# Attention output projections with every load begun at once, and attention cores whose first loads stand ahead of the clearing

## The reference

```python
attn = jax.nn.softmax(attn.astype(jnp.float32), axis=-1).astype(q.dtype)
ctx = jnp.einsum('bhqk,bhkd->bhqd', attn, v)
ctx = ctx.transpose(0, 2, 1, 3).reshape(B, N, D)
return ctx @ Wo + bo          # layer 1: out @ w_o.T * hid ** (-0.5), no bias
```

## Time and profile before

| what | value |
|---|---|
| median of 3 runs | 3518.85 us (3512.96 to 3518.86) |
| the profiled execution | 3530.75 us, its span 3529.0 us |
| mean granted TensorE clock | 0.886 of full speed |
| busy over the span | PE 77%, DVE 71%, ACT 52%, POOL 25% |
| first attention core | 125.1 to 802.4 us |
| first output projection | 807.15 to 855.77 us |
| second attention core | 1270.7 to 1947.3 us |
| second output projection | 1951.97 to 2000.73 us |

### The profile page before, as it was taken

One profiled execution on the slowest core, in us unless ns is written; L12 is line 12 of the kernel. 1 busy time (PEld: TensorE's weight loads), 2 busy tenths in 40 slices (PEclk: granted clock), 3 DMA queues, 4 the chain that ended last, 5 costly groups with the idle time before them and its releaser, 6 DMA issues. The chain is left out here.

```text
span 3529.0 us, 43620 instructions
## 1 busy us (share of the span) xinstructions
PE 2701.9 (77%) x12690; PEld 967.9 (27%) x12690; DVE 2505.7 (71%) x2942; ACT 1823.1 (52%) x3161; POOL 882.6 (25%) x985
## 2 busy tenths in 40 slices
PE   6499999984469649999998424867777777996666
PEld 3022222221136412222222114622222232332222
DVE  4699999963236469999996271288999975446548
ACT  2188888881224128888888102355555531224233
POOL 3311111100446221111110006416777740000000
PEclk8599999996789759999999657987999998998878
DMA  4200101003522330100100312111000000001010
GB/s 120 91 24 23 28 23 28 23 15 89 90 70 67 106 117 24 28 24 24 27 23 15 102 35 74 48 51 38 6 12 12 7 0 1 0 0 59 6 42 24
DMA packets 161483, 140.96 MB, mean 40 GB/s; under 512 B 51941, under 2 KB 135781, under 8 KB 160984
## 3 DMA queue, kind: packets, MB, share of 16 engines
q1 hardware_dynamic: 142040, 98.68, 10.5%
q0 software_dynamic: 19328, 40.87, 3.8%
HBM read 73.85 MB, written 65.62 MB: 40 GB/s over the span
## 5 line engine op out<-in xcount | busy, mean ns | idle before, releaser
L640 DVE TENSOR_REDUCE a_att_mx<-a_att_s 128x2 f32<-128x1024 f32 x1024 | 1204.9, 1219 | 77.8 <-PE a_att_s L551 65.7
L625 ACT ACTIVATE a_att_pt<-a_att_st 128x512 f32<-128x512 f32 x2048 | 1064.5, 603 | 246.9 <-PE a_att_st L577 246.3
L577 PE MATMUL a_att_st<-a_att_qst,a_att_kst 50*128 50x512 bf16 x2048 | 620.7, 385 | 63.9 <-ACT a_att_pt L625 51.6
L551 PE MATMUL a_att_s<-a_att_kst,a_att_qst 50*128 50x512 bf16 x2048 | 524.8, 399 | 85.1 <-DMA a_att_kst<-a_kstk 52.2
L564 PE MATMUL a_att_av<-a_att_pt,a_att_vst 128*32 128x512 f32 x4096 | 547.2, 607 | 0.0
L577 PEld LDWEIGHTS a_att_st<-a_att_qst,a_att_kst 50*128 50x128 bf16 x2048 | 157.9, 94 | 727.1 <-ACT a_att_pt L625 668.7
L2191 POOL TENSOR_TENSOR g_xn<-m2s_hs,m2s_cb 128x1024 f32<-128x1024 f32 x128 | 300.8, 2355 | 119.0 <-DVE m2s_hs L2158 68.7
L2158 DVE TENSOR_TENSOR_SCAN m2s_hs<-m2s_da,m2s_bps 128x1024 f32<-128x1024 f32 x128 | 292.7, 2287 | 4.4
L487 POOL CAST a_att_mt_in<-a_att_nmax 128x16 bf16<-128x16 f32 x64 | 12.6, 196 | 1072.7 <-DVE a_att_nmax L648 1072.7
L2074 PE MATMUL m2s_yps<-g_xn,g_ident 128*128 128x512 f32 x512 | 242.8, 597 | 0.9
L2130 ACT COPY m2s_cb<-m2s_cps 128x1024 f32<-128x1024 f32 x128 | 129.5, 1012 | 184.1 <-POOL g_xn L2191 182.5
(11 more groups left out here) (477 smaller groups left out, 3681.5 us busy)
## 6 DMA issues: line engine op xcount, KB each, us to landing
a_att_qst<-a_qstk POOLq DMA_DIRECT2D x128, 100.0 KB, 2.5
a_att_kst<-a_kstk POOLq DMA_DIRECT2D x128, 100.0 KB, 2.6
a_qstk<-a_qkv_part SPq DMA_DIRECT2D x96, 128.0 KB, 1.9
a_kstk<-a_qkv_part SPq DMA_DIRECT2D x96, 128.0 KB, 2.0
f_xs<-f_sent SPq DMA_DIRECT2D x20, 396.0 KB, 5.8
f_sent<-f0r_zero SPq DMA_DIRECT2D x1, 5148.0 KB, 22.7
a_num<-a_att_oev SPq DMA_DIRECT2D x256, 16.0 KB
a_out_nm<-a_num SPq DMA_DIRECT2D x16, 256.0 KB, 3.4
```

Source lines behind the costliest of these rows:

```text
L551: mm = pe.matmul(s1[:, cut % 2, h, :], qst[u][64 * h:64 * h + STACK, qt * P:(qt + 1) * P], kst[u][64 * h:64 * h + STACK, kh * CH:(kh + 1) ...
L577: pe.matmul(st[:, e % 3, :], kst[u][64 * h:64 * h + STACK, kt * P:(kt + 1) * P], qst[u][64 * h:64 * h + STACK, half * CH:(half + 1) * CH], ...
L625: act.activation(pt[:, e % 16, :], st[:, e % 3, :], ACT.Exp, scale=scale).then_inc(exp_done, 1)
L640: dve.tensor_reduce(mx[:, par, 2 * cut:2 * cut + 2], s1[:, cut % 2, :, :], AX.X, ALU.max).then_inc(s1_used, 1)
```

## The change

1. Output projection. `nm` and `cx` are gone; the numerators are loaded into `g.xn` by four transfers of 1024 tokens each (512 KB), issued by ScalarE, whose stream was empty in this stage. They wait for nothing. `rb` has a buffer for every chunk, and SP issues its 8 loads one behind the other, with no wait between them, once the reciprocals are stored. The loop is written out. DVE multiplies in place in `g.xn` and does the addition of chunk c-2 behind the multiplication of chunk c; PE has 4 PSUM banks where it had 2. Each load has its own semaphore: the stage has 18 where it had 8.
2. Attention core. Two of pair 0's four stacks (head 0's) are loaded by SP, the other two and those of pairs 1 and 2 by POOL at the very start, ahead of the clearing of `vst`; the three copies of values stand behind the clearing. PE's first cut waits for SP's two on a semaphore of their own and for POOL's two on `ldq[0]`.

```diff
@@ attention_stage
+                for hp in range(3):
+                    for h in range(2):
+                        if hp > 0 or h == 1:
+                            stacks(pool, 0, hp, h, ldq[hp])
                 for u in range(4):
                     pool.memset(vst[u][:, :, :, :], 0.0).then_inc(vset, 1)
...
                 for hp in range(3):
-                    fetch(0, hp, None)
+                    values(0, hp)
...
+                stacks(sp, 0, 0, 0, ldq_first)
                 for n in range(2):
                     rows(n, n, 16 * (n // 2 + 1))
...
                     if cut == 0:
-                        pe.wait_ge(ldq[u], 64 * rounds)
+                        if isinstance(n, int) and n == 0:
+                            pe.wait_ge(ldq_first, 32)
+                        pe.wait_ge(ldq[u], 64 * rounds - (32 if u == 0 else 0))
@@ out_proj_stage, SP
-                with sp.Fori(0, NCH // 2) as m:
-                    for u in range(2):
-                        sp.wait_ge(ctx_ready, 2 * m)
-                        sp.dma_start(nm[:, u, :], num[:, chunk(2 * m + u)]).then_inc(cl[u], 16)
-                        sp.dma_start(rb[:, u, :], by_chunk[m, u].unsqueeze(1).to_broadcast([HEADS, HD, CH])
-                                     ).then_inc(cl[u], 16)
+                for c in range(NCH):
+                    sp.dma_start(rb[:, c, :], by_chunk[c // 2, c % 2].unsqueeze(1).to_broadcast([HEADS, HD, CH])
+                                 ).then_inc(rb_here[c], 16)
+            @block.scalar
+            def _(act):
+                for i in range(4):
+                    act.dma_start(g.xn[:, 2 * i * CH:2 * (i + 1) * CH], num[:, 2 * i * CH:2 * (i + 1) * CH]).then_inc(num_here[i], 16)
@@ out_proj_stage, DVE
+                def weigh(c):
+                    dve.wait_ge(rb_here[c], 16)
+                    dve.wait_ge(num_here[c // 2], 16)
+                    dve.tensor_tensor(g.xn[:, cols(c)], g.xn[:, cols(c)], rb[:, c, :], ALU.mult).then_inc(ctx_ready, 1)
...
+                for c in range(NCH):
+                    weigh(c)
+                    if c >= 2:
+                        add(c - 2)
+                add(NCH - 2)
+                add(NCH - 1)
@@ out_proj_stage, PE
+                for c in range(NCH):
+                    pe.wait_ge(ctx_ready, c + 1)
+                    if c >= 4:
+                        pe.wait_ge(added, c - 3)
+                    pe.matmul(ps[:, c % 4, :], wo[:, :], g.xn[:, cols(c)], start=True, stop=True).then_inc(proj_ready, 1)
```

More of the change, by code:

```diff
@@ L460, in attention_stage, with stacks @@
         UNITS, CUTS = 32, 16
+        ldq_first = s.sem("ldq_first")
+        def stacks(engine, b, hp, h, landed):
+            for t, src in ((qst[hp % 4], qstk), (kst[hp % 4], kstk)):
+                engine.dma_start(t[64 * h:64 * h + STACK, :], src[:, 2 * hp + h, bass.ds(b * SEQ, SEQ)]).then_inc(landed, 16)
         with nc.Block() as block:
@@ L699, in _ @@
                 sp.dma_start(dn[:, :], den).then_inc(dl, 16)
-                for weights in ahead:
-                    weights.load(sp)
                 sp.wait_ge(rdone, 1)
```

57 lines of the change are left out of this document (24 added, 33 removed).

## The result

The changed kernel takes 3454.74 us, the median of 4 runs (3453.1 to 3473.03); the kernel before, on the same chip, 3515.9 us (3502.75 to 3518.86, 4 runs). The ratio is 0.9843, with a 95% interval of 0.9813 to 0.9874: 1.6% faster (the two medians by themselves give 1.7%). The forecast was 3465.9 us in a range of 3450 to 3483. The profiled execution took 3454.14 us, where the one of before took 3530.75: 76.6 us less, of which the stages that the change touches give 52.

The account below looks back on a forecast made before the run. No engine is full; a chain of stages and latencies bounds the kernel. Projections 44.0, cores 6.6 and normalizations 2.4 make 53.0 us, taken off the median 3518.85: 3465.9 us, range 3450 to 3483.

Parts of the forecast that it names:

- The loop: Output projections, first multiplication to last addition: DVE sets the pace if PE keeps up, 12.7 and 12.3 us.
- chunk 2 at 0.74 + 3.6 = 4.34, and its addition can start at 6.56: Projection loop: PE starts cold at 1.8 us a chunk, so chunk 2's addition can start 6.56 us after the first multiplication.
- Rival 1: PE stays at half clock in both projections and into the normalizations: 3475.5 us; chance 0.14.
- The head: Projection, denominators' issue to first multiplication: 0.55 us gained, numerators' traffic costs 1.2, so 0.7 us later.
- I take +0.7, the value with both queues served in turn: Projection head: denominators and numerators pass in turn, slowed and not blocked, so the first multiplication comes 0.7 us later.
- Rival 2: Projection heads: the denominators wait for all the numerators, a delay of about 6 us, giving 3476.5 us; chance 0.12.
- rival 4: Projections: broadcast loads served one at a time, 4.5 us each, loop 35.2 us, 15.3 added to head: 3542 us; chance 0.02.
- The starts of the cores: Attention cores: first stacks issued at the release let PE start 3.4 and 3.2 us earlier, together 6.6.
- Rival 3: Core starts: first stacks come no earlier, because SP is late or ten transfers crowd them: 3472.5 us; chance 0.05.
- The normalizations: Normalizations behind the projections: a warmer PE clock gives back 2.4 us of a possible 4.1.
- The sum: Whole kernel: projections 44.0, cores 6.6 and normalizations 2.4 us, together 53.0 us less.
- First multiplication 13 to 15 us behind the issue of the denominators: Sign expected in the trace after, at the projection's head: first multiplication 13 to 15 us behind that issue.

Follow-up runs that it names:

- the alternating loop: Changed kernel with each addition straight behind its product, all loads still issued at once: 3540.77 us, ratio 0.9986 to the kernel before.
- experiment with pair 0 alone: Changed kernel with only pair 0's two POOL stacks ahead of the clearing, pairs 1 and 2 behind it: 3453.26 us, ratio 0.9829 to the kernel before.

## Where the prediction was right and where not

**What bounds the kernel.** Right: no engine's busy time changed by more than 21 us in 2700 (TensorE's; 6.8 of them in the first projection, 16.59 to 9.75, where its clock now rises), and the time fell with the waits. The chain of latencies of the earlier trace rows was the thing to shorten.

**The loop: 12.7 and 12.3 us forecast, 11.39 and 11.27 measured.** The mechanism was right: three products, then additions and products in turn on a full VectorE. The step that was too dear is PE's: "chunk 2 at 0.74 + 3.6 = 4.34, and its addition can start at 6.56". It took half clock for the first two chunks and more, and the clock was already at 0.75 in 824 to 826: chunk 2's addition started at 826.80, 5.54 us behind the first product. From the first addition on VectorE ran through: 8 additions and 5 products from 824.19 to 832.65, 0.65 us each, where 0.67 and 0.69 had been taken. Rival 1, half clock all through, is out; in the alternating loop (28.3 us) PE idles 1.44 us of every 3.52 and the granted clock stays at 0.50, and with the stagger, which takes these idle times away, it rose.

**The head: +0.7 us forecast, +3.0 and +2.5 measured.** This is the step that failed: "I take +0.7, the value with both queues served in turn". Denominators took 7.21 and 7.27 us to land, 4.45 and 4.56 more than before, and not 1.2. The sum has turns from the first moment, at the best rate. In the trace the queues do take turns, but late: first the denominators stand still for 2.4 us longer than before, a wait that the sum does not have, and then the turns cost 2.1 us, not 1.2. With the numerators held back the landing is 2.76 again; with 512 KB ahead instead of 2 MB it is 3.5 and 3.2. Why a transfer that is issued 1.2 us behind others moves nothing for 3.35 us is open; it isn't that they first had to end, since half of the numerators were still to pass. By the prediction's own sign, "if the reciprocal starts 6 us or more behind the issue of the denominators", its account of the head is wrong.

Two small things gave time back: the first load of reciprocals is issued 2.02 us behind the store instead of 2.92, and lands and is used after 3.58 instead of 4.12. 4.45 - 0.90 - 0.54 = 3.0. The forecast had 0.55 for both.

Rival 2, "the denominators wait for all the numerators", comes nearer: +6 us to the landing, where 4.5 were measured, and a landing near the end of the numerators' traffic. In 12 projections of six kernels' runs with all four loads at the start, the denominators landed up to 0.7 us before the last numerators had passed (in two of them at the same moment, within 0.1). But it has the way wrong: they didn't wait for all, since from 808.4 on both moved. A faster rate would not have mended its sum. 2.3 MB at the 426 GB/s of a weight load in the earlier trace rows are 5.4 us and a delay of 2.7; that this is near the head's +3.0 is a coincidence, since 1.44 us of the 4.45 came back elsewhere. The 412 GB/s are the rate of the fullest stretch; between 804.9 and 812.8 all together moved at about 300. Nor do the rivals add up: 1 and 2 together would be 3486, above the range's end of 3483.

The store of reciprocals takes 2.0 us to land in both kernels, and behind the first, only the second broadcast was waited for in the first projection (0.61 us) and the second and third in the other (0.28 and 0.30). So rival 4, which would have made the kernel slower, is out.

The prediction weighed two rules of the Trainium skill here, from "DMA: Bandwidth & Descriptors". The first, in "Issuing engines are not separate DMA queues", that transfers of different issuers run on the same 16 engines, is borne out: the second issuer hid nothing of the bandwidth. The second, in "Queues, rings and completion order", that each of the engines goes round the queues packet by packet, agrees with the second part of the delay only: from 808.5 to 810.5 the trace has 119 packets of the denominators' queue beside 157 of the numerators'. It says nothing of the first part, in which an issued transfer moved no packet. A price worked out from turns alone was 1.2 us, and 4.45 were measured.

**The starts of the cores: 3.4 and 3.2 us forecast, 2.7 and 2.5 measured.** Right in kind. Two sizes were off by a half microsecond. "POOL's first issue is now at the release": it came 0.56 us behind ScalarE's first instruction (125.72 to 126.28), and the last of the four stacks needed 3.3 to 3.5 us to the first cut (127.03 to 130.39) where 2.66 was taken from the earlier trace rows. The experiment with pair 0 alone does not settle how much of it the other eight transfers cost. The rule of the Trainium skill, in "DMA: Bandwidth & Descriptors", section "Latency and other measured facts", of a first byte sooner on the sync queue than on GpSimd's, agrees with the trace: SP's first packet moves 0.93 us behind its issue and POOL's 1.41. It gave no time, since PE waits for all four stacks and the last to be issued was POOL's. Rival 3 is out.

**The normalizations: 2.4 us forecast, 4.35 measured.** Both column means took the 5.42 us of a warm start, so the clock stayed through the gap at both: the upper end, 4.1, was the true one. The first stage gave 3.63 and the second 0.72, since the whole of a normalization whose means take 5.42 us is 21.05 us long in some executions, 22.00 in others and up to 22.3 in single ones, whatever the kernel. So 4.35 against 4.1 is partly luck. The choice of "a little over half" between "stays" and "falls" had no row behind it.

**The sum: 53.0 us forecast, 51.9 in the touched stages.** That the two are so near is luck, because the errors cancel: head 4.1 dearer than forecast in two projections, loops 2.3 cheaper, cores 1.4 dearer, normalizations 1.9 cheaper. With the median of before as it stands with a fourth run, 3515.9 - 51.9 = 3464.0 would be the time, and the median measured is 9.3 below it; those lie in stages that vary by themselves. Two kinds of such variation are shown in the same code: the first mixture at 272 to 274 or at 300 to 310 us, and the last pairs of a core at a granted clock of 1.00 or of 0.50 to 0.75, up to 17 us.

**What was named as a sign.** "First multiplication 13 to 15 us behind the issue of the denominators" was wrong (16.2); landings about 1 us apart, the full VectorE, the length (27.6 and 27.5 instead of 26 to 27), the clock and the 5.4 us were right or nearly; PE's first cut came 4.7 us behind the release instead of 4.

## What to carry to other kernels

When a stage is a chain of latencies, price it wait by wait: early loads alone gave 7 us here, the stagger alone 16, both 24, and neither touched an engine's busy time. A bulk load issued just ahead of a small one that the chain waits for delays the small one by microseconds though it is in another engine's queue (4.5 us here for 2 MB, 0.5 to 0.8 for 512 KB), and by more than a fair share of the bandwidth would cost. Putting it behind the small one only passed the delay to the next transfer of the chain; what took it away here was to move three quarters of the bulk load into the stage before. When a landing is late, look at the view of the queues: it tells a transfer that has not begun from one that shares the engines. And a stage's time in one profile is compared with the same stage in another execution of the same kernel before a difference is explained by the change.

## What the runs showed of the hardware

- A load of 256 KB on one queue, issued 1.2 us behind 2 MB on another, landed in 7.2 us (6.4 to 7.4 in the other runs) where it takes 2.7 alone: its first packet moved 3.35 us behind its issue instead of 1.0, and its packets then took 3.5 us instead of 1.4. 256 KB stored beside 2 MB took 5.96 us from issue to what follows it instead of 2.02; beside 512 KB the load took 3.2 to 3.5.
- Plain rows of 4 KB moved at 412 GB/s in this place, with all transfer engines full.
- The granted clock went from 0.50 to 1.00 within 4 us of the first matmul when matmuls followed each other without a gap, and stayed at 0.50 over a whole projection when PE idled 1.44 of 3.52 us.
- It also fell to 0.50 at the end of an attention core in 4 of the 13 profiled executions, one core of the two each time (of the kernel before, of the changed one and of two variants), with PE busy 17.94 of 20 us; the same code ran at 1.00 in the others, busy 16.09. The cause is open.
- In the first mixture VectorE shows idle times of 24 and 32 us that end in "issue" or "remote", in some executions and on some chips, and not in others. Their cause is open.
